# A decoder layer's feed-forward: the down projection of three chunks by seven half-size products, its sums accumulated in DRAM by transfers

## The chip, the cores and the metric

One NeuronCore of a Trainium2 chip runs the whole program. The metric is the device time of one execution in microseconds (us), the median of the runs. Engines are named as the profile names them: PE is TensorE, DVE is VectorE, ACT is ScalarE, POOL is GpSimd, SP is SyncE, which here only issues transfers.

## The reference

A decoder layer over x of 8 x 100 tokens by 1024, all in float32: a retention block, a cross attention with 722 context positions, and a gated feed-forward of hidden width 4096, each followed by an addition of the residual and a layer normalisation. The change touches the feed-forward, whose input x is the normalised output of the attention block:

```
h   = silu(x @ w_gate.T) * (x @ w_up.T)        # 800 x 4096
y   = x + h @ w_down.T                         # 800 x 1024
out = layernorm(y)
```

## The kernel before, in words

Everything is kept transposed: a tensor of 800 tokens by 1024 features stands as 128 partitions x 8 tiles (k) x 800 columns. A float32 product is made of three matmuls in fp32r: weights and operand are split into a high part (ACT copies, rounding) and a low part (DVE subtracts the high part from the original), and PE multiplies high x high, high x low and low x high.

The feed-forward (`phase_tail`, from line 3368) goes over 4 chunks of 1024 hidden features (`CHUNKS`). A chunk has two stages.

*Gate and up* (56 products, lines 3641 to 3684). The chunk's 8 tiles of hidden features are made in four couples of two; a couple takes a gate block (even block b) and an up block (odd b). Each block is a 2 x 2 block product by the seven-product scheme of Strassen and Winograd: 7 products, each of 4 k-tiles x 3 passes = 12 matmuls of 400 columns (`QUAD = 4`, `HALF = 400`), in place of 8. The moving operands (`MOVING`) are quarters of x and four sums of quarters ("sides"), made once. The stationary ones are quarters of a pair of weight units in `RAW`, and sums of them, made by DVE ("mixes", line 3958, four a block). What PE is given as weights are "entries": 512 columns of high part made by ACT (line 3821) and of low part by DVE (line 4062), in a ring of four slots. So the entry of product n may be begun when product n - 4 is done. The results stand in three PSUM banks a block, and are put together by DVE with five additions ("combines": u2, u3, c22, c21, c12, line 4105) and one ACT copy (`keep`, line 3873). Products 4, 6 and 7 open or add to a bank that an earlier combine or keep must have read. ACT applies silu (line 3867), DVE multiplies gate by up (m11, m22, m21, m12, line 4119). The result G (two tiles x 800) is split into `HH` (ACT, line 3852) and `HL` (DVE, line 4073), the hidden operand.

*Down* (lines 3700 to 3717). Eight output units, each of 8 k-tiles x 2 column parts (512 and 288 columns) x 3 passes = 48 matmuls, plain. DVE adds each unit's two banks to the residual `c.R` in SBUF (line 4134). Weight units are split whole, 1024 columns at a time (lines 3838, 4068). The last chunk's down stage goes by halves of the columns, interleaved with the closing normalisation (`down_by_halves`); it is another function.

Nothing is planned by a scheduler: each engine has its list of instructions written out by hand in `chunk` (PE line 3742, ACT line 3875, DVE line 4158), executed strictly in that order, with waits on counting semaphores (`f_hi`, `f_lo` for entries, `f_done` for products, `outs` for combines and multiplications, `kept`, `h_hi`, `h_lo`, `t_sum`, `t_hi`, `t_lo`). SP issues the load of each pair of weight units (1 MB, line 3516) when the low part of an entry two pairs back is made. POOL does nothing in the feed-forward but one memset (line 3505). In the retention phase POOL issues transfers that add in place (line 1716), as it does for the value weights (`add_raw`, line 112).

Of the kernel before, what the change touches and what calls it, by code (L numbers as in the profile page):

```python
# [65 lines left out]
ENTRIES = 8 * PRODUCTS + 2 * KT  # L66
# [103 lines left out]
def phase_context(c, nc, sem):  # L170

    with ExitStack() as ctx:
# [1123 lines left out]
        done.wv_mix = wv_mix  # L1296
        c.minus, c.MINUS = wv_hi, 8
# [232 lines left out]
def phase_retention(c, nc, sem, before, norm):  # L1530


    with ExitStack() as ctx:
# [135 lines left out]
        def sync(sp):  # L1669
# [1698 lines left out]
def phase_tail(c, nc, sem_of, attention):  # L3368
# [4 lines left out]
    with ExitStack() as ctx:  # L3373
# [5 lines left out]
        def below(words, *tiles, dtype=F32):  # L3379

            with ExitStack() as room:
# [17 lines left out]
        kept_parts.append(below("t_wo6_", (FLAT, UNIT), (0, UNIT), dtype=F32R))  # L3399
        ROOM = sb("ROOM", [P, AFTER], F32R)  # L3400
        G = sb("G", [P, 2, NT])
        U2, U3, CT = (sb(n, [P, HALF]) for n in ("U2", "U3", "CT"))
        S3 = sb("S3", [P, QUAD * P])
        (x_hi, x_lo, added, gated, freed, h_hi, h_lo, stored, f_hi, f_lo, f_done, s_op, outs, silu,
         t_sum, t_hi, t_lo, r_add, ones_made, kept) = (sem(n) for n in (
             "x_hi", "x_lo", "added", "gated", "freed", "h_hi", "h_lo", "stored", "f_hi", "f_lo",
             "f_done", "s_op", "outs", "silu", "t_sum", "t_hi", "t_lo", "r_add", "ones_made", "kept"))
# [26 lines left out]

        MOVING = (operand(0, 0), side(2), side(1), side(3), operand(1, 0), side(4), operand(1, 1))
        BANK = (0, 1, 2, 1, 0, 1, 2)
        OPENS = (True, True, True, True, False, True, False)

# [5 lines left out]
        def block_source(b, p):  # L3444

            if p == 3:
                return S3[:]
            return raw_pair(b)[:, (0, 0, 2, None, 1, 3, 1)[p], :]
# [7 lines left out]

        def down_unit(t, n):
            if t == LAST:
                return last_down(n)
            return c.WH[:, n % 2, :], c.WL[:, n % 2, :]  # L3460
# [42 lines left out]
        def gpsimd(pool):  # L3503
            pool.wait_ge(f_done, PER * LAST + 56)
            pool.memset(ones[:], 1.0 / D).then_inc(ones_made, 1)

        def sync(sp):
            weight_stream(c, sp, U_WO // 2 + 2, (U_FFN - U_WO) // 4 + 1)

            def load(t, i):  # L3510

                before = (PER * t + 7 * (i - 1) if 2 <= i < 10 else
                          PER * t + 56 + 4 * (i - 9) if i >= 10 else
                          PER * t - 4 * (2 - i) + 4)
# [3 lines left out]

            def chunk(t, first, last):
# [10 lines left out]
            sp.wait_ge(stored, 16 * KT)  # L3530
# [59 lines left out]
        def tensor(pe):  # L3590
# [50 lines left out]
            def product(t, b, p, first):  # L3641
                couple, up = b // 2, b % 2
                base = 14 * couple + 5 * up
                if p == 0:
# [10 lines left out]
                    if first and b == 2:  # L3655
                        pe.wait_ge(gated, 2)
# [804 lines left out]
```

## Time and profile before

| | us |
|---|---|
| median of 3 runs (lowest, highest) | 2628.17 (2628.12, 2628.95) |
| the profiled execution, its own time | 2627.58 |
| its span in the profile | 2625.8 |
| PE busy | 2593.7 (99%) |
| DVE busy | 1811.0 (69%) |
| ACT busy | 1200.9 (46%) |
| POOL busy | 24.2 (1%) |

The span is the stretch from the first to the last instruction of the profiled execution; its own time is 1.8 us more. Matmul records are pipelined and overlap, so the pace of PE is the distance between starts, not the mean duration of a record. The feed-forward's chunks begin at about 1867, 2030.7, 2223.0 and 2415.4 us; the first has only six blocks, since its first couple is made before it.

### The profile page before, as it was taken

The numbers are of one execution on the slowest core, as the hardware profiler recorded it, in microseconds if no ns is written. First come the engines' busy times: TensorE is split into PE (matmuls) and PEld (weight loads), VectorE is DVE, ScalarE is ACT, GpSimd is POOL, SyncE is SP. The second block draws the span as 40 slices with busy tenths as digits, with TensorE's granted clock in tenths as the row PEclk, the third lists the DMA queues.
The fourth block names the chain that finished last, engine by engine and source line by source line (L and its number), as shares of the span: only waits on it lengthen the run. The fifth ranks groups of instructions, "written<-read, shape, count | busy, mean of one in ns | idle before, by whom it ended". The sixth has DMA issues, their size and how long they took to land.

```text
span 2625.8 us, 41672 instructions
## 1 busy us (share of the span) xinstructions
PE 2593.7 (99%) x16328; PEld 2458.0 (94%) x16328; DVE 1811.0 (69%) x2502; ACT 1200.9 (46%) x2047; POOL 24.2 (1%) x37
## 2 busy tenths in 40 slices
PE   9999999999999999999999999999999999999998
PEld 9999999999999988998889999899998999999997
DVE  7777776687777764867788888736973763763766
ACT  6555555555444433444466666522531431431441
POOL 0000000000000000000000000000000000000000
PEclk9999999999999999999999999999999999999999
DMA  5444445422212231344256666421121121211121
GB/s 198 159 145 161 149 135 179 148 78 60 73 57 77 62 90 52 94 106 93 75 143 174 174 170 166 106 76 55 47 81 48 65 81 49 81 65 65 65 80 51
DMA packets 138765, 264.79 MB, mean 101 GB/s; under 512 B 25076, under 2 KB 98284, under 8 KB 125676
## 3 DMA queue, kind: packets, MB, share of 16 engines
q1 hardware_dynamic: 136108, 255.53, 31.5%
q0 software_dynamic: 2496, 7.01, 1.5%
q8 instruction: 113, 1.85, 0.3%
q14 instruction: 48, 0.39, 0.0%
HBM read 198.24 MB, written 57.26 MB: 97 GB/s over the span
## 4 chain that ended last, share of the span: by engine, by line
PE 94%; DVE 3%; ACT 1%; issue 1%; DMA 0%; DVEq 0%; POOL 0%; SPq 0%; ACTq 0%; POOLq 0%
PE PS L3680 6%; PE PS L3678 6%; PE PS L3682 6%; PE PS L3151 5%; PE PS L149 4%; PE PS L147 4%; PE PS L148 4%; PE PS L2526 3%; PE PS L2528 3%; PE PS L2524 3%; PE PS L3164 3%; PE PS L1181 3%; PE PS L1183 3%; PE PS L1185 3%; PE PS L1144 3%; PE PS L1146 3%
## 5 line engine op out<-in xcount | busy, mean ns | idle before, releaser
L3821 ACT ACTIVATE WH<-RAW 128x512 fp32r<-128x512 f32 x180 | 113.5, 632 | 222.1 <-PE PS L3682 119.4
L149 PE MATMUL PS<-XH,WL 128*128 128x512 f32 (+1 forms) x592 | 204.4, 345 | 0.0
L147 PE MATMUL PS<-XH,WH 128*128 128x512 f32 (+1 forms) x592 | 204.1, 345 | 0.0
L4062 DVE TENSOR_TENSOR WL<-RAW,WH 128x512 fp32r<-128x512 f32 x196 | 134.7, 688 | 58.8 <-ACT WH L3821 55.5
L148 PE MATMUL PS<-XL,WH 128*128 128x512 f32 (+1 forms) x496 | 170.1, 343 | 0.0
L3680 PE MATMUL PS<-XL,WH 128*128 128x400 f32 x480 | 166.0, 346 | 0.0
L3678 PE MATMUL PS<-XH,WH 128*128 128x400 f32 x480 | 164.8, 343 | 0.8 <-issue 0.6
L3682 PE MATMUL PS<-XH,WL 128*128 128x400 f32 x480 | 165.0, 344 | 0.0
L3323 DVE TENSOR_TENSOR XL<-PS,XH 128x400 fp32r<-128x400 f32 (+2 forms) x224 | 122.6, 571 | 56.3 <-ACT XH L3256 51.7
L3256 ACT ACTIVATE XH<-PS 128x400 fp32r<-128x400 f32 (+2 forms) x224 | 106.4, 507 | 95.9 <-PE PS L3164 95.9
L1745 ACT ACTIVATE WH<-RAW 128x512 fp32r<-128x512 f32 x132 | 81.8, 632 | 132.3 <-DVE RAW L2046 79.5
L3716 PE MATMUL PS<-t_ROOM,WL 128*128 128x512 f32 (+1 forms) x384 | 132.5, 345 | 0.0
L3715 PE MATMUL PS<-t_ROOM,WH 128*128 128x512 f32 (+1 forms) x384 | 131.7, 343 | 0.0
L3714 PE MATMUL PS<-t_ROOM,WH 128*128 128x512 f32 (+1 forms) x384 | 131.6, 343 | 0.0
L3304 DVE TENSOR_REDUCE a_LOW<-PS 100x1 f32<-100x824 f32 x128 | 129.7, 1014 | 2.5
L3678 PE MATMUL PS<-t_ROOM,WH 128*128 128x400 f32 x360 | 124.4, 345 | 0.3 <-issue 0.3
L1181 PE MATMUL PS<-WALL,WH 128*128 128x256 f32 x448 | 124.5, 278 | 0.0
L1183 PE MATMUL PS<-WALL,WL 128*128 128x256 f32 x448 | 124.3, 277 | 0.0
L1185 PE MATMUL PS<-WALL,WH 128*128 128x256 f32 x448 | 124.2, 277 | 0.0
L3680 PE MATMUL PS<-t_ROOM,WH 128*128 128x400 f32 x360 | 124.1, 345 | 0.0
L3682 PE MATMUL PS<-t_ROOM,WL 128*128 128x400 f32 x360 | 123.9, 344 | 0.0
L149 PEld LDWEIGHTS PS<-XH,WL 128*128 128x128 f32 x592 | 111.3, 188 | 12.3
(536 smaller groups left out, 8168.7 us busy)
## 6 DMA issues: line engine op xcount, KB each, us to landing
RAW<-weights_dram SPq DMA_DIRECT2D x100, 1024.0 KB, 4.9
values_scratch<-VS SPq DMA_DIRECT2D x44, 512.0 KB
a_KHL<-keys_scratch SPq DMA_DIRECT2D x32, 411.0 KB, 5.1
RAW<-context_dram SPq DMA_DIRECT2D x6, 2048.0 KB, 8.9
XH<-values_scratch SPq DMA_DIRECT2D x16, 640.0 KB
XL<-values_scratch SPq DMA_DIRECT2D x16, 640.0 KB
R<-context_dram SPq DMA_DIRECT2D x4, 2048.0 KB, 9.3
keys_scratch<-KS SPq DMA_DIRECT2D x16, 512.0 KB, 3.9
```

Source lines behind the costliest of these rows:

```text
L147: pe.matmul(out, wh, xh[:, k, cols], start=(k == 0), stop=False)
L148: pe.matmul(out, wh, xl[:, k, cols], start=False, stop=False)
L149: mm = pe.matmul(out, wl, xh[:, k, cols], start=False, stop=(k == KT - 1))
L1181: pe.matmul(out, hi[:, k, cols], wh, start=(opens and t + k == 0), stop=False, skip_group_check=True)
L1183: pe.matmul(out, lo[:, k, cols], wh, start=False, stop=False, skip_group_check=True)
L1185: mm = pe.matmul(out, hi[:, k, cols], wl, start=False, stop=(k == QUAD - 1), skip_group_check=True)
L3678: pe.matmul(out, wh, high[:, k, :], start=(OPENS[p] and k == 0), stop=False, skip_group_check=True)
L3680: pe.matmul(out, wh, low[:, k, :], start=False, stop=False, skip_group_check=True)
L3682: mm = pe.matmul(out, wl, high[:, k, :], start=False, stop=(k == QUAD - 1), skip_group_check=True)
L3715: pe.matmul(out, wh, HL[:, k, cols], start=False, stop=False)
L3716: mm = pe.matmul(out, wl, HH[:, k, cols], start=False, stop=(i == KT - 1))
L4062: dve.tensor_tensor(ring[1][:, e % RING, :], src, ring[0][:, e % RING, :].bitcast(F32), ALU.subtract).then_inc(f_lo, 1)
```

## The change

In chunks 0, 1 and 2 the down projection becomes four blocks (`DOWN_BLOCKS`) of seven products each, through the same function as the gate and up blocks (`strassen`), with the same ring of entries and the same mixes of weights. Its moving operands (`HIDDEN`) are quarters of the hidden operand and four sums of them, made per couple by DVE (`hidden_sum`), then split by ACT (`hidden_side_hi`) and DVE (`hidden_side_lo`). Sums 1 need the first two couples, sums 2, 3 and 4 the last two. A down block's results are put together by three ACT copies (`keep_down`) and five DVE additions (`combine_down`) in G, two tiles x 800.

The place of the residual in SBUF is needed for the sums: `c.HSIDE` has the addresses of `c.R`. So the normalised x is stored to DRAM (`rscr`) by SP (`keep_residual`), each down block's two tiles are added to it there by accumulating transfers that POOL issues (`send`), and before the last down stage it is fetched back (`fetch_residual`). G is free for the next block when the transfer has landed (`SENT`). u2 and u3 of the gate blocks now stand in U2 and U3 instead of G.

In the retention phase a load of SP gets one wait more. The last chunk's gate, up and down stages do the work of before.

```
+DOWN_BLOCKS = KT // 2
+BLOCKS = 8 + DOWN_BLOCKS
-ENTRIES = 8 * PRODUCTS + 2 * KT
+ENTRIES = BLOCKS * PRODUCTS
...
                 sp.wait_ge(f_lo, F_LO + PER * (i - 1) + 14)
+                sp.wait_ge(roped, 2 * i + 1)
                 load_pair(pair_of(i, 3))
...
+        HIDDEN = (hidden(0, 0), hidden_side(2), hidden_side(1), hidden_side(3), hidden(1, 0),
+                  hidden_side(4), hidden(1, 1))
+        DOWN_ORDER = (0, 2, 1, 4, 3, 6, 5)
...
+            def send(t, d, tile):
+                if t == 0 and d == 0:
+                    pool.wait_ge(stored, STORED)
+                if t > 0 or d > 0:
+                    pool.wait_ge(SENT[tile], sent(t, d - 1, tile))
+                pool.dma_start(c.rscr[:, 2 * d + tile, :], G[:, tile, :],
+                               accum_op=ALU.add).then_inc(SENT[tile], 16)
+            for t in range(LAST):
+                for d in range(DOWN_BLOCKS):
+                    pool.wait_ge(kept, down_kept(t, d, 3))
+                    pool.wait_ge(outs, down_outs(t, d, 4))
+                    send(t, d, 0)
+                    pool.wait_ge(outs, down_outs(t, d, 5))
+                    send(t, d, 1)
...
+            def fetch_residual():
+                sp.wait_ge(f_done, PER * LAST)
+                for tile in range(2):
+                    sp.wait_ge(SENT[tile], sent(LAST - 1, DOWN_BLOCKS - 1, tile))
+                for k in range(0, KT, 2):
+                    sp.dma_start(c.R[:, k:k + 2, :], c.rscr[:, k:k + 2, :]).then_inc(stored, 16)
             def chunk(t, first, last):
                 for i in range(4 if first else 0, 12):
+                    if last and i == 4:
+                        fetch_residual()
                     load(t, i)
+            keep_residual()
...
+            def down_product(t, d, q):
+                if q == 0:
+                    if d == 0:
+                        pe.wait_ge(h_lo, KT * t + 4)
+                        pe.wait_ge(outs, OUTS * t + (14 * 3 + 5))
+                        pe.wait_ge(silu, 16 * t + 14)
+                    elif d == 1:
+                        pe.wait_ge(outs, OUTS * t + GATES)
+                    else:
+                        pe.wait_ge(outs, down_outs(t, d - 2, 5))
+                        pe.wait_ge(kept, down_kept(t, d - 2, 3))
+                if q == 3:
+                    pe.wait_ge(kept, down_kept(t, d, 1))
+                if q == 4:
+                    pe.wait_ge(outs, down_outs(t, d, 1))
+                if q == 5:
+                    pe.wait_ge(kept, down_kept(t, d, 2))
+                if q == 6:
+                    pe.wait_ge(outs, down_outs(t, d, 2))
+                if d == 0 and q == 3:
+                    pe.wait_ge(h_lo, KT * t + KT)
+                if d == 0 and q in (1, 2, 4, 6):
+                    pe.wait_ge(t_lo, side_parts(t, {1: 2, 2: 6, 4: 7, 6: 8}[q]))
+                strassen(t, 8 + d, q, HIDDEN)
...
+            def keep_down(t, d, which):
...
+                    act.wait_ge(f_done, PER * t + (56 + PRODUCTS * d + 4))
+                    if d == 0:
+                        act.wait_ge(t_sum, side_sums(t, SUMS))
+                        act.wait_ge(h_lo, KT * t + KT)
+                    else:
+                        act.wait_ge(SENT[0], sent(t, d - 1, 0))
+                    out, x = G[:, 0, 0:HALF], bank(0)
...
+            def combine_down(t, d, which):
...
+                elif which == "u3":
+                    dve.wait_ge(f_done, PER * t + at + 5)
+                    dve.wait_ge(outs, down_outs(t, d, 1))
+                    out, x, y = U3[:], U2[:], bank(1)
...
```

DVE's list in a gate block that follows a finished couple (`ended`), and in the down stage:

```
                     entry_lo(t, e)
-                    if inner and not up:
-                        hidden_lo(t, couple - 1, 1)
+                    if not last and ended in (0, 1):
+                        hidden_sum(t, 1, ended)
+                    if not last and ended == 2:
+                        hidden_sum(t, 2, 2)
+                    if ended is not None:
+                        hidden_lo(t, ended, 1)
                     entry_lo(t, e + 1)
                     if not (first and b == 2):
                         mix(t, b, 3)
-                    if inner and not up:
-                        hidden_lo(t, couple - 1, 0)
+                    if not last and ended == 2:
+                        hidden_sum(t, 3, 2)
                     combine(t, b, "u2")
...
                         entry_lo(t, e + 2)
+                        if not last and ended == 2:
+                            hidden_sum(t, 4, 2)
+                        if ended is not None:
+                            hidden_lo(t, ended, 0)
...
+                    for d in range(DOWN_BLOCKS):
...
+                        if d == 0:
+                            last_part(t, 7)
+                            hidden_sum(t, 2, 3, 0)
+                            hidden_sum(t, 3, 3, 0)
+                            hidden_sum(t, 4, 3)
+                            hidden_side_lo(t, 2, 3)
+                            entry_lo(t, e)
+                            hidden_lo(t, 3, 1)
+                            hidden_lo(t, 3, 0)
+                            entry_lo(t, e + 1)
+                            combine_down(t, d, "u2")
+                            hidden_side_lo(t, 3, 3)
+                            mix(t, b, 3)
+                            entry_lo(t, e + 2)
+                            hidden_side_lo(t, 4, 3)
+                            entry_lo(t, e + 3)
+                            mix(*following, 0)
+                            mix(*following, 1)
+                        else:
+                            combine_down(t, d - 1, "c21")
+                            entry_lo(t, e)
+                            entry_lo(t, e + 1)
+                            mix(t, b, 3)
+                            mix(*following, 0)
+                            mix(*following, 1)
+                            entry_lo(t, e + 2)
+                            combine_down(t, d, "u2")
+                            entry_lo(t, e + 3)
+                        entry_lo(t, e + 4)
+                        mix(*following, 2)
+                        combine_down(t, d, "u3")
+                        combine_down(t, d, "c22")
+                        entry_lo(t, e + 5)
+                        combine_down(t, d, "c12")
+                        entry_lo(t, e + 6)
```

Later in a gate block come the lows of the sides: `hidden_side_lo(t, 1, ended)` after couples 0 and 1, `hidden_side_lo(t, 2, 2)`, `(t, 3, 2)` and `(t, 4, 2)` in block 6; in block 7 the sums 2 and 3 of the last couple's second tile. ACT's list has the matching high parts, `keep_down` "u", "ct" and "c11" ahead of a down block's entries 1, 2 and 4, and in block 0 of the down stage `hidden_hi(t, 3, 1)`, the entry, `hidden_side_hi(t, 2, 3)`, `hidden_hi(t, 3, 0)`, then one side high after each of the next two entries.

## Rows read from the trace of the kernel before

**Rows 1.** The page, part 1: engines, busy us, share of the span, instructions.

```profile
PE 2593.7 (99%) x16328; PEld 2458.0 (94%) x16328; DVE 1811.0 (69%) x2502; ACT 1200.9 (46%) x2047; POOL 24.2 (1%) x37
```

**Rows 2.** Table by stage: chunk 1's products, then its down projection.

```profile
core 0: us, PE busy (x) PEld busy (x) DVE busy (x) ACT busy (x) POOL busy (x), PEclk, DMA share, GB/s
2030.68:2153.40 122.72, 122.72 (x674) 122.28 (x673) 92.61 (x147) 50.40 (x87) 0.00 (x0) 1.00 0.20 69
2153.40:2223.03 69.63, 69.63 (x386) 61.45 (x385) 21.11 (x23) 9.80 (x11) 0.00 (x0) 1.00 0.18 61
```

**Rows 3.** Waits of PE, 1867 to 2538: who waited for whom, us, times, longest.

```profile
PE PS L3678 <- issue: 0.8, 2, 0.6
PE PS L3678 <- DVE WL L4062: 0.2, 1, 0.2
```

**Rows 4.** Groups by line and form, chunk 1: busy, mean ns | idle before.

```profile
L4062 DVE TENSOR_TENSOR WL<-RAW,WH 128x512 fp32r<-128x512 f32 x52 | 35.8, 688 | 16.4 <-ACT WH L3821 15.5
L3958 DVE TENSOR_TENSOR RAW<-RAW 128x512 f32<-128x512 f32 x24 | 16.6, 692 | 0.8
L4105 DVE TENSOR_TENSOR t_G<-t_G,PS 128x400 f32<-128x400 f32 x16 | 9.1, 571 | 6.1 <-PE PS L3682 5.9
L4073 DVE TENSOR_TENSOR t_ROOM<-t_G,t_ROOM 128x800 fp32r<-128x800 f32 x8 | 7.8, 985 | 0.0
...
L3852 ACT ACTIVATE t_ROOM<-t_G 128x800 fp32r<-128x800 f32 x8 | 6.8, 860 | 0.0
```

**Rows 5.** Timeline of DVE from the end of block 5: start, us, what.

```profile
2122.90 0.57 DVE L4105 TENSOR_TENSOR t_CT<-t_U,PS 128x400 f32<-128x400 f32 x1 [0.42 <-PE PS L3682]
2123.51 0.57 DVE L4119 TENSOR_TENSOR t_G<-t_CT,t_G 128x400 f32<-128x400 f32 x1
...
2127.48 0.98 DVE L4073 TENSOR_TENSOR t_ROOM<-t_G,t_ROOM 128x800 fp32r<-128x800 f32 x1
2128.59 0.57 DVE L4105 TENSOR_TENSOR t_G<-t_U,PS 128x400 f32<-128x400 f32 x1
2129.08 0.69 DVE L4062 TENSOR_TENSOR WL<-RAW,WH 128x512 fp32r<-128x512 f32 x1
2129.68 0.68 DVE L3958 TENSOR_TENSOR t_S<-RAW 128x512 f32<-128x512 f32 x1
2130.40 0.69 DVE L3958 TENSOR_TENSOR RAW<-RAW 128x512 f32<-128x512 f32 x1
...
2131.71 1.18 DVE L4105 TENSOR_TENSOR t_G<-t_G,PS 128x400 f32<-128x400 f32 x2
...
2155.30 1.89 DVE L4073 TENSOR_TENSOR t_ROOM<-t_G,t_ROOM 128x800 fp32r<-128x800 f32 x2
```

**Rows 6.** Timeline of PE, block 6: first two matmuls of product 4.

```profile
2129.25 0.42 PE L3678 MATMUL PS<-t_ROOM,WH 128*128 128x400 f32 x1
2129.51 0.34 PE L3680 MATMUL PS<-t_ROOM,WH 128*128 128x400 f32 x1
```

**Rows 7.** DMA issues: KB each, median us to landing; last, line 1716's own.

```profile
RAW<-weights_dram SPq DMA_DIRECT2D x100, 1024.0 KB, 4.9
a_KHL<-keys_scratch SPq DMA_DIRECT2D x32, 411.0 KB, 5.1
...
VW<-RAW POOLq DMA_DIRECT2D x4, 512.0 KB, 4.6
...
keys_scratch<-KS SPq DMA_DIRECT2D x4, 420.0 KB, 3.3
...
DMA to landing us min/median/max: 3.1/3.6/7.2
```

**Rows 8.** Timelines of SP, POOL and DVE, retention, first head loop.

```profile
574.51 0.33 SPq L1677 DMA_DIRECT2D RAW<-weights_dram  x1
...
570.91 1.80 POOL L1716 DMA_DIRECT2D T<-T  x2 [569.75 <-DVE T L2118]
...
584.47 0.68 DVE L2046 TENSOR_TENSOR S<-RAW 128x512 f32<-128x512 f32 x1
```

More of the change, by code:

```diff
@@ L3913, in chunk @@
                                 gate(t, couple, "s11")
-                if last:
-                    act.preload_act_table_set("natural_log_exp_and_others")
-                for n in range(2 * KT if last else KT):
+                if not last:
+                    for d in range(DOWN_BLOCKS):
+                        for q in range(PRODUCTS):
+                            if q == 0 and d == 0:
+                                hidden_hi(t, 3, 1)
+                            if q == 1:
+                                keep_down(t, d, "u")
+                            if q == 2:
+                                keep_down(t, d, "ct")
+                            if q == 4:
+                                keep_down(t, d, "c11")
+                            entry_hi(t, 56 + PRODUCTS * d + q + 3)
+                            if q == 0 and d == 0:
+                                hidden_side_hi(t, 2, 3)
+                                hidden_hi(t, 3, 0)
+                            if d == 0 and q in (1, 2):
+                                hidden_side_hi(t, q + 2, 3)
+                    return
+                act.preload_act_table_set("natural_log_exp_and_others")
+                for n in range(2 * KT):
                     if n == 0:
@@ L4173, in chunk @@
                     inner = b > (2 if first else 0)
-                    ahead = b < 7
+                    ahead = b < 7 or not last
+                    ended = couple - 1 if inner and not up else None
                     e = PRODUCTS * b + 3
                     if b == 0:
-                        add_rows(t - 1, KT - 1)
-                        entry_lo(t, 2)
+                        combine_down(t - 1, DOWN_BLOCKS - 1, "c21")
                     if inner:
@@ L4216, in chunk @@
                         times(t, couple, "m22")
+                        if not last and couple == 3:
+                            hidden_sum(t, 2, 3, 1)
+                            hidden_sum(t, 3, 3, 1)
+                        if first and b == 3:
+                            for each in range(2):
+                                first_hidden_sum(each)
+                    elif not last and ended in (0, 1):
+                        hidden_side_lo(t, 1, ended)
+                    elif not last and ended == 2:
+                        hidden_side_lo(t, 2, 2)
                     entry_lo(t, e + 5)
@@ L4220, in chunk @@
                         times(t, couple, "m21")
-                    entry_lo(t, e + 6)
+                        if first and b == 3:
+                            hidden_side_lo(t, 1, 0)
+                    elif not last and ended == 2:
+                        hidden_side_lo(t, 3, 2)
+                        hidden_side_lo(t, 4, 2)
+                    entry_lo(t, e + 6)
+                if not last:
+                    for d in range(DOWN_BLOCKS):
+                        b, e = 8 + d, 56 + PRODUCTS * d + 3
+                        following = (t, b + 1) if d < DOWN_BLOCKS - 1 else (t + 1, 0)
+                        if d == 0:
[16 more added lines that the diff above has]
+                            mix(*following, 1)
+                        else:
+                            combine_down(t, d - 1, "c21")
[14 more added lines that the diff above has]
+                        entry_lo(t, e + 6)
+                    return
                 last_part(t, 7)
```

459 lines of the change are left out of this document (282 added, 177 removed).

## The prediction

> **What bounds the kernel now.** The page's engine line [rows 1] has TensorE busy 99% of the span and VectorE 69%. A busy PE is not a PE at its peak, so the table by stage is read next. It is cut at the starts of chunk 1's first gate product, its first down matmul and the next chunk's first product: the gate and up products take 122.72 us, the down projection 69.63 us [rows 2]. In both PE is busy throughout at a granted clock of 1.00, the higher of its two levels; the other engines differ: VectorE is busy 75% of the first stretch and 30% of the second. The waits of PE over all four chunks' products hold 1 us [rows 3]. So TensorE's own pace is the bound, and VectorE is the engine with the least room.
>
> The pace comes from the length of these stretches, not from mean durations, since pipelined records overlap. 122.72 us for 56 products of 12 matmuls is 0.1826 us per 128x400 matmul and 2.19 us per product; 69.63 us for 384 matmuls averaging 400 columns is 0.1813 us each.
>
> **TensorE's part.** Per chunk 0 to 2 the 384 down matmuls (8 units x 8 k x 2 column parts x 3 passes) become 4 blocks x 7 products x 4 k x 3 passes = 336 matmuls of 400 columns. They issue from the statement that the gate products issue from, so they cost 336 x 0.1826 = 61.4 us against 69.6: 8.3 us less a chunk, 24.8 us in three, if nobody is late. Weight loads fall 384 to 336 with the columns, 400 to a load before and after. Chunk 3 keeps its down projection.
>
> **What VectorE and ScalarE get in exchange.** Added per chunk on VectorE: 28 low entries and 16 mixes of 512 columns, 20 combines of 400, 10 operand sums and 8 operand lows of up to 800; gone are 4 + 6x2 half-unit lows and 8 row adds of 800. By durations [rows 4] the new chunk holds about 157 us of VectorE work (84 entries 58, 48 mixes 33, 76 ops of 400 43, 4 hidden lows of 400 and 4 of 800 6, ten sums 8, eight side lows 8), where now it is busy 93 + 21 = 114 us, in 184 us of PE time. On average it fits. What decides is where it stands, because a chunk's sums can only be made when its last couples are done.
>
> I step through the queues by the distance of neighbouring starts, not by durations, since the records overlap by about 0.08 us: 0.49 us for a 400 op and 0.61 when the next one needs its result; 0.60 and 0.72 for a 512 op; 0.90 and 1.11 for an 800 op [rows 5]. A product may start without a gap if what it waits for ended 0.39 us before the signal of the product ahead. That comes from one row pair: the combine ("u2") at 2128.59 ended at 2129.15; the product that waits for its bank has its first two matmuls 0.26 us apart instead of 0.18, so it is 0.08 late, while the product ahead signals at 2122.90 + 3 x 2.19 = 2129.46 [rows 5, 6]; 2129.15 + 0.39 - 2129.46 = 0.08.
>
> Block 6 (clock 0 = end of block 5, products end every 2.19). Before its second combine ("u3") VectorE now has: c12 and m12 1.1, entry 0.6, a sum 0.9, hidden low 0.9, entry 0.7, mix 0.6, second sum 0.9, u2 0.5, entry 0.6, third sum 0.9, hidden low 0.9, two mixes 1.3, entry 0.6. u3 starts at 10.6 and ends at 11.1; before it started at 8.8 [rows 5]. The sixth product wants its bank at 10.95 - 0.39: about 0.5 us lost. Block 7, with two 400 sums, gains it back in its own waits, and VectorE enters the down stage 0.4 us late.
>
> Down block 0 (clock 0 = end of block 7). VectorE: c12, m12, two single-tile sums, one 800 sum; the low of side 2 starts at 3.7 and ends at 4.7. ScalarE has its high part by 3.1, so it is not late. The third product wants it at 4.38 - 0.39: 0.7 us lost. Two hidden lows follow, ended at 7.1 where the fourth product wants them at 6.9: 0.2 us. Then entry, u2, side 3's low, mix, an entry that waits 0.7 us for ScalarE's high part, side 4's low, entry, two mixes, entry, mix: u3 starts near 15.3 and ends at 15.9, while the seventh product wants its bank at 13.6 (six products, the 0.9 us lost so far, less 0.39): 2.3 us. Together 3.2 us. Blocks 1 to 3 carry 7 entries, 4 mixes, 5 combines, 10.4 us in 15.3, and lose nothing; block 0 of the next chunk likewise. Blocks 2 and 4 trade an 800 low before u2 for a sum and a 400 low and lose nothing. Against the 0.1 us a block like 6 loses already, a chunk loses 3.6 us, three lose 10.8. ScalarE itself is busy 50 of 123 us [rows 2]; its additions (12 keeps, 8 side highs of up to 0.86 [rows 4], 12 more half-entries net) fit, but its queue is in order, which matters below.
>
> **The accumulating transfers.** No row shows one that ends in DRAM. Nearest are 512 KB sums in SBUF, 4.6 us to landing, and 200 KB ones, 3.1 to 7.2 us; a plain 420 KB store took 3.3 us, a plain 411 KB load 5.1 us [rows 7]. The new ones carry 400 KB. Lower bound 3.3 us, upper 7.2 us, or the load and the store one after the other, 8.4 us; I take 5 us, nearest the 512 KB rows. They have cover: tile 0 is complete 0.6 us after the sixth product and is wanted by ScalarE (c11) after the next block's fourth, 10.9 - 0.6 = 10.3 us; tile 1 has about 11 us, and 8.2 us at the end of a chunk, where the gate block's combines come earlier. Behind a late c11 stands that block's next high entry, with 1 us to spare. So up to 8.2 us the price is nothing, and at 8.4 us still nothing that is seen.
>
> The Trainium skill, "Collectives: The Full Stack", section on why ReduceScatter is half of AllGather, says an adding transfer reads two sources and so moves its bytes at half the rate. The 512 KB sum above took 4.6 us where a plain load of 1024 KB took 4.9 [rows 7], so this case's trace agrees about the rate; and if the rule is laid on the 411 KB load it gives an estimate of 10.2 us, with which the sum would still be what it is, the cover nearly used up.
>
> **The rest.** The 8 residual stores leave SP's queue after the normalised tiles and ahead of the load of pair 4, which anyhow waits for the seventh entry of block 2; weights arrive in 4.9 us against a 15 us block [rows 7]. The fetch of 3.2 MB stands ahead of pair 4 in chunk 3, with two blocks of slack, and is used 120 us later. Price nothing; if the cover were gone, 17 us once (four loads like the 4.9 us one, one by one, less overlap). The new wait on the first head loop's fourth load: the load went out at 574.51, the sum behind its wait was issued at 570.91 and lands about 3.6 later, so the load goes 1 us late, is 5 us long and is first read at 584.47 [rows 7, 8]. Nothing.
>
> **Sum.** 2627.58 us of the profiled execution (span 2625.8 and 1.8 around it) - 24.8 + 10.8 = 2613.6. The profiled execution is 0.6 us under the median of the runs, so 2614.2 as a median.
>
> **Rivals.**
> (1) All of it is hidden, the gain is 24.8 us: 2603.4. For it: the ring of four entries lets VectorE be up to 4.9 us late with an entry (three products, less 1.3 us to make it and the 0.39). Against: u3 and side 2's low are not entries, they have one product of slack. Chance 0.12.
> (2) VectorE's queue costs twice what I step through (a stall in block 6 carried into block 7 and the down stage): 3 x 7.2 = 21.6 us back, 2625.0, within what can be told apart from no change. Chance 0.08.
> (3) Slower: the accumulating transfer is the new bound. Place: ScalarE's c11 in down blocks 1 to 3, and VectorE's c22 in the next chunk's block 0; both stand at the head of in-order queues with the entries behind them. With landing time L it costs 9 x (L - 11.3) + 3 x (L - 11.0); it cancels my gain of 14.0 us at L = 12.3. At three times the 512 KB row, 13.8 us, it costs 31 us: 2645. Against it: every transfer row is under 8. Chance 0.06.
> The forecast holds 0.74, from 2608 (stalls of 1.5 us a chunk) to 2621 (6 us).
>
> **Numbers.** 0.2% is 5.3 us, about what a measurement of this kernel can tell from no change. Faster 0.88 (forecast, rival 1 and the good edge of rival 2), same 0.06, slower 0.06. The range 2603 to 2622 takes in rival 1 and leaves out (2)'s centre and (3).
>
> **What would show it.** Gate stretches as now near 122.7 us plus 0.5; down stretches of chunks 0 to 2 near 64.6 us, of which 61.4 PE; PE waits of some 0.7 and 2.3 us in the third and seventh product of down block 0, released by VectorE (the low of side 2, then u3); no wait of ScalarE on the transfers. Landing times over 11 us, or down stretches over 69 us, make it wrong; stretches of 61.5 us make rival 1 right.

## The result, and the profile after

The changed kernel takes 2611.06 us (median of 4 runs, 2610.54 to 2611.18); the kernel before took 2628.14 us on the same chip (4 runs, 2627.91 to 2628.95). The ratio is 0.9935, 95% interval 0.9922 to 0.9947: 17.1 us less. The forecast was 2614.2 us, 3.1 us above it. As the following shows, several things that the forecast did not have lie behind that small difference, and the two largest, both of them effects outside the products themselves, point in opposite directions.

First the page of the kernel after, its engine line and the transfers of the residual. They answer to [rows 1] and [rows 7].

```profile
PE 2573.4 (99%) x16184; PEld 2459.5 (94%) x16184; DVE 1912.8 (73%) x2695; ACT 1258.6 (48%) x2168; POOL 45.0 (2%) x61
...
residual_scratch<-t_G POOLq DMA_DIRECT2D x24, 400.0 KB, 5.1
```

TensorE has 144 matmuls fewer (3 x 48) and is still busy 99%; VectorE has 193 instructions and 102 us more. The time lies where it lay before, in TensorE's pace, so the next view is the table by stage: chunk 1's products and its down projection, answering to [rows 2], and four short stretches that the text comes to.

```profile
core 0: us, PE busy (x) PEld busy (x) DVE busy (x) ACT busy (x) POOL busy (x), PEclk, DMA share, GB/s
2022.56:2145.62 123.06, 122.87 (x673) 122.35 (x673) 100.22 (x161) 53.62 (x93) 0.96 (x2) 1.00 0.23 76
2145.62:2211.40 65.78, 63.45 (x338) 62.42 (x338) 47.31 (x75) 26.00 (x45) 6.01 (x7) 0.97 0.44 102
...
1974.00:1977.60 3.60, 3.60 (x13) 3.60 (x12) 2.44 (x5) 0.63 (x1) 0.86 (x1) 0.53 0.36 28
...
2159.30:2161.80 2.50, 0.49 (x4) 0.16 (x2) 2.33 (x4) 1.15 (x2) 0.00 (x0) 1.00 0.90 259
2161.80:2165.30 3.50, 3.50 (x11) 3.46 (x12) 2.26 (x4) 0.11 (x1) 0.86 (x1) 0.51 0.27 115
...
2350.60:2354.00 3.40, 3.40 (x19) 3.40 (x20) 3.12 (x6) 0.76 (x2) 0.94 (x2) 1.00 0.27 113
```

The gate and up stretch grew by 0.34 us (forecast 0.5). The down stretch fell from 69.63 to 65.78 us (forecast near 64.6), and its mean granted clock is 0.97 instead of 1.00. That third number had no place in the forecast.

Who is late for whom is in the waits of PE from 1860 to 2540 us, which answer to [rows 3] (waiting engine, released by; us in total, times, longest):

```profile
PE PS L3740 <- DVE t_U L4348: 6.0, 3, 2.0
PE PS L3740 <- DVE HSIDE L4272: 1.0, 3, 0.3
...
PE PS L3740 <- DVE t_U L4311: 0.7, 4, 0.2
```

The stalls have the names and the places that were forecast: u3 (line 4348) 2.0 us once in each of three chunks, the low of side 2 (line 4272) 0.3, and block 6's second combine (line 4311, three times). The fourth wait on line 4311 has no place in the forecast: in chunk 0, block 3, the fourth product waits for the first combine (u2), and its start at 1886.10 us comes 0.51 us behind the one before. The recorded wait is shorter than the loss, because the record before it still runs. The loss is read from starts: in the timeline of PE the third and the seventh product of chunk 1's down block 0.

```profile
2149.80 0.34 PE L3744 MATMUL PS<-HSIDE,WL 128*128 128x400 f32 x1
2150.47 0.45 PE L3740 MATMUL PS<-HSIDE,WH 128*128 128x400 f32 x1 [0.32 <-DVE HSIDE L4272]
2150.76 0.34 PE L3742 MATMUL PS<-HSIDE,WH 128*128 128x400 f32 x1
...
2159.36 0.34 PE L3744 MATMUL PS<-t_ROOM,WL 128*128 128x400 f32 x1
2161.72 0.60 PE L3740 MATMUL PS<-t_ROOM,WH 128*128 128x400 f32 x1 [2.01 <-DVE t_U L4348]
2162.12 0.54 PE L3742 MATMUL PS<-t_ROOM,WH 128*128 128x400 f32 x1
2162.45 0.54 PE L3744 MATMUL PS<-t_ROOM,WL 128*128 128x400 f32 x1
```

Starts are 0.67 us and 2.36 us apart where 0.18 to 0.19 is the pace: 0.48 and 2.17 us lost. The start after such a one is late too, here by another 0.11 us (0.29 apart). Behind the long gap the next starts are 0.40 and then 0.33 us apart instead of 0.18. This is the lower level of the clock: the stretch from 2161.80 has a granted clock of 0.51 with TensorE busy throughout, the 2.50 us ahead of it 1.00 with TensorE nearly idle. Chunk 0 shows the same (1974.00, clock 0.53), there from about 1.2 us after TensorE went on at 1972.88; chunk 2 has a gap of the same size, and none of it (2350.60, clock 1.00).

The timeline of DVE in the same block tests the step through its queue (clock 0 of the forecast is 2146.0):

```profile
2156.17 0.69 DVE L4218 TENSOR_TENSOR WL<-RAW,WH 128x512 fp32r<-128x512 f32 x1 [0.76 <-ACT WH L3925]
...
2158.45 0.69 DVE L4117 TENSOR_TENSOR t_S<-RAW 128x512 f32<-128x512 f32 x1
2159.16 0.69 DVE L4117 TENSOR_TENSOR RAW<-RAW 128x512 f32<-128x512 f32 x1
2159.78 0.68 DVE L4218 TENSOR_TENSOR WL<-RAW,WH 128x512 fp32r<-128x512 f32 x1
2160.49 0.69 DVE L4117 TENSOR_TENSOR RAW<-RAW 128x512 f32<-128x512 f32 x1
2161.10 0.56 DVE L4348 TENSOR_TENSOR t_U<-t_U,PS 128x400 f32<-128x400 f32 x1
```

u3 starts 15.1 us after the clock 0, where 15.3 was forecast; the entry's wait for ScalarE is 0.76 us (0.7 forecast). Right ahead of u3 stand three mixes for the next block, which nobody wants yet.

**The part outside the feed-forward.** Its first product starts at 1862.14 us, before at 1867.27: 5.1 us of the gain are there before any changed product has run. They come in the main from one place near 940 us, the last head loop of the retention phase. Waits of all engines from 900 to 970 us, before:

```profile
ACT QK L1804 <- POOLq L1719: 8.2, 1, 8.2
...
PE PS L2385 <- DVE R L2135: 4.5, 1, 4.5
```

The same view after:

```profile
ACT QK L1808 <- POOLq L1723: 4.1, 1, 4.1
...
PE PS L2389 <- DVE R L2139: 0.3, 1, 0.3
```

And the issues there, from the timelines of SP and POOL, before:

```profile
933.18 0.33 SPq L1677 DMA_DIRECT2D RAW<-weights_dram  x1
...
932.81 0.83 POOL L1716 DMA_DIRECT2D T<-T  x1 [2.53 <-issue]
```

and after:

```profile
937.01 7.81 SPq L1680 DMA_DIRECT2D RAW<-weights_dram  x2
...
933.81 0.83 POOL L1720 DMA_DIRECT2D T<-T  x1 [2.54 <-issue]
```

Before, SP sent a 1 MB weight load 0.4 us behind POOL's 200 KB sum, and the sum landed after 7.2 us, the maximum of line 1716 in [rows 7]. After, the added wait holds the load back until the sum has landed, which takes 3.1 us, and ScalarE, VectorE and TensorE behind it go on 4 us earlier.

The wait is not the whole price. Behind the 4.5 us gap of the kernel before stands the lower clock, in a view of PE alone:

```profile
core 0: us, PE busy (x), PEclk, DMA share, GB/s
946.70:951.20 4.50, 4.50 (x14) 0.51 0.87 230
```

The 13 starts from 946.68 to 951.18 us take 4.50 us, where the same shapes (six of 512 columns, six of 288, one of 512) take 2.41 at the pace of the rows around them: 2.1 us more. The kernel after has clock 1.00 there. So the place is worth 4.1 us of gap and 2.1 us of clock, 6.2 us. Of these 5.1 are left at the first product because the profiled execution of the kernel after came to this place 1.0 us later than that of the kernel before (938.67 against 937.68 us, the first matmul on PE's line 2389, before 2385); it is there at the first accumulating sum already (571.91 against 570.91 us), ahead of the added wait's first use, and it differs between executions: run 3, whose program is the same up to there, reaches the later place at 937.96 us.

### The profile page after: what moved, and what is told of

Read it like the earlier page. It is cut to its first block, busy times and chain, and to the rows that moved or that the text cites. A ratio compares the mean times of both kernels' runs of the same rounds, so it can differ in the third digit from the quotient of the medians.

```text
span 2608.9 us, 42024 instructions
## 1 busy us (share of the span) xinstructions
PE 2573.4 (99%) x16184; PEld 2459.5 (94%) x16184; DVE 1912.8 (73%) x2695; ACT 1258.6 (48%) x2168; POOL 45.0 (2%) x61
## 4 chain that ended last, share of the span: by engine, by line
PE 90%; DVE 6%; issue 2%; ACT 1%; DMA 0%; DVEq 0%; POOL 0%; SPq 0%; ACTq 0%; POOLq 0%
PE PS L3740 7%; PE PS L3742 7%; PE PS L3744 7%; PE PS L3155 5%; PE PS L151 4%; PE PS L149 4%; PE PS L150 4%; PE PS L2530 3%; PE PS L2532 3%; PE PS L2528 3%; PE PS L3168 3%; PE PS L1183 3%; PE PS L1185 3%; PE PS L1187 3%; PE PS L1146 3%; PE PS L1148 3%
## 5 line engine op out<-in xcount | busy, mean ns | idle before, releaser
L3925 ACT ACTIVATE WH<-RAW 128x512 fp32r<-128x512 f32 x252 | 158.5, 630 | 253.2 <-PE PS L3744 168.3
L4218 DVE TENSOR_TENSOR WL<-RAW,WH 128x512 fp32r<-128x512 f32 x256 | 176.0, 688 | 61.8 <-ACT WH L3925 56.3
L3740 PE MATMUL PS<-t_ROOM,WH 128*128 128x400 f32 x552 | 191.9, 348 | 6.5 <-DVE t_U L4348 6.0
L3742 PE MATMUL PS<-t_ROOM,WH 128*128 128x400 f32 x552 | 191.5, 347 | 0.0
L3744 PE MATMUL PS<-t_ROOM,WL 128*128 128x400 f32 x552 | 191.0, 346 | 0.0
L1749 ACT ACTIVATE WH<-RAW 128x512 fp32r<-128x512 f32 x132 | 81.8, 631 | 130.4 <-DVE RAW L2050 74.0
L102 DVE TENSOR_TENSOR WL<-RAW,WH 128x1024 fp32r<-128x1024 f32 x40 | 49.0, 1225 | 104.5 <-ACT WH L96 100.1
L151 PEld LDWEIGHTS PS<-XH,WL 128*128 128x128 f32 x592 | 111.3, 188 | 12.3
L1146 PE MATMUL PS<-WH,WALL 128*128 128x256 f32 x440 | 122.7, 279 | 0.0
L1148 PE MATMUL PS<-WL,WALL 128*128 128x256 f32 x440 | 122.5, 279 | 0.0
```

Source lines behind the costliest of these rows:

```text
L151: mm = pe.matmul(out, wl, xh[:, k, cols], start=False, stop=(k == KT - 1))
L1146: pe.matmul(out, wh, hi[:, k, :], start=(opens and j + k == 0), stop=False, skip_group_check=True)
L1148: pe.matmul(out, wh, lo[:, k, :], start=False, stop=False, skip_group_check=True)
L3740: pe.matmul(out, wh, high[:, k, :], start=(OPENS[p] and k == 0), stop=False, skip_group_check=True)
L3742: pe.matmul(out, wh, low[:, k, :], start=False, stop=False, skip_group_check=True)
L3744: mm = pe.matmul(out, wl, high[:, k, :], start=False, stop=(k == QUAD - 1), skip_group_check=True)
```

## The experiments

**1 and 2. The retention wait alone, both ways.** Theory: the added wait in the retention phase is worth 5 us by itself. Rival: the 5 us belong to something else of the change. First the kernel before with the wait added:

```diff
                 sp.wait_ge(f_lo, F_LO + PER * (i - 1) + 14)
+                sp.wait_ge(roped, 2 * i + 1)
                 load_pair(pair_of(i, 3))
```

> The kernel before with one line more: the load of the fourth weight pair of each head loop in the retention phase waits for the rotation of that loop's first tile. Theory A (the wait keeps a 1 MB weight load from getting in front of an accumulating transfer in the last head loop, where the trace of before shows 7.2 us to landing and a 4.5 us stall of TensorE, and the trace of after neither): 2628.1 - 5.1 = 2623.0 us, and the 4.5 us stall gone. Rival B (the 5.1 us by which the changed kernel reaches its feed-forward earlier come from the moved memory or semaphores, not from the wait): 2628 us, stall unchanged. Rival C (what I had forecast, the wait costs and gains nothing): 2628 us as well.

Measured: 2622.15 us (10 runs) against 2628.23 (14 runs), ratio 0.9976 (0.9967 to 0.9986), 6.1 us less. TensorE's wait from 900 to 970 us:

```profile
PE PS L2386 <- DVE R L2136: 0.3, 1, 0.3
```

The converse, the kernel after without that line:

> The changed kernel without that one wait. Theory A: the 4.5 us stall of TensorE at the last head loop comes back, 2611.1 + 5.1 = 2616.2 us, and the feed-forward itself is as in the changed kernel, 11.8 us shorter than before. Rivals B and C: 2611 us. If both e1 and e2 move by 5 us, the parts add up and the down projection's own gain is 12 us, not 17.

Measured: 2616.77 us (5 runs), ratio 0.9957 (0.9943 to 0.997), 5.7 us more than the kernel after. TensorE's wait from 900 to 970 us, and below it the table by stretches, behind the long gap of chunk 0, then behind that of chunk 2:

```profile
PE PS L2388 <- DVE R L2138: 4.5, 1, 4.5
```

```profile
1979.50:1982.50 3.00, 3.00 (x11) 2.96 (x10) 1.60 (x4) 0.15 (x1) 0.86 (x1) 0.50 0.26 31
...
2354.70:2357.70 3.00, 2.98 (x9) 2.95 (x10) 2.26 (x4) 0.21 (x1) 0.65 (x1) 0.54 0.33 139
```

Added to one kernel or taken from the other, the wait moves the same 4 us of waits and 5.7 to 6.1 us of time; the rest is the clock behind the gap, which has 0.50 at 946 to 950 us in run 2 and 1.00 in run 1. That is shown. The second table adds that here the lower clock stands behind the gaps of chunks 0 and 2; in the kernel after it was chunks 0 and 1. The gaps are the same 2 us, so length alone does not decide it.

**3. The long gap closed.** In down block 0, u3, an entry and c22 go ahead of the three mixes.

```diff
                             entry_lo(t, e + 3)
-                            mix(*following, 0)
-                            mix(*following, 1)
+                            combine_down(t, d, "u3")
+                            entry_lo(t, e + 4)
+                            combine_down(t, d, "c22")
+                            for n in range(3):
+                                mix(*following, n)
```

> The changed kernel with VectorE's list in down block 0 reordered: u3, the next entry and c22 stand ahead of the three mixes. Theory D (the seventh product waits 2.2 us for u3, behind work that is not urgent, and the gap also lowers the granted clock to 0.5 for 3.4 us in two of three chunks, 1.6 us each): 3 x 2.2 + 2 x 1.6 = 9.8 us less, 2601.3 us, and no stretch under clock 1.00 in the down stages. Rival E (the clock falls there whatever the gap): 3 x 2.2 = 6.6 us less, 2604.5, the half-clock stretches remain. Rival F (VectorE is overloaded in that block, so the time comes back at the next wait): 2608 or more.

Measured: 2600.41 us (2600.22 to 2600.6, 4 runs), ratio 0.9894 (0.9879 to 0.9909). In the waits of PE the line of u3 is gone, what is left is as before:

```profile
PE PS L3740 <- DVE HSIDE L4272: 1.0, 3, 0.3
```

10.7 us less than the kernel after, for 6.0 us of recorded waits (6.5 by starts, 6.8 with the late start behind each). 3.3 us of the rest is the clock, whose lower stretches are gone: its mean over the core goes from 0.997 to 0.999. Another 0.8 us has nothing to do with the edit: the same product of chunk 0 starts at 1868.31 us here and at 1869.11 in the kernel after, before either has done anything different.

**4. The other stalls too.** Run 3, and in block 6 the third sum behind an entry and the fourth behind c22, in down block 0 the third sum behind the hidden lows (the counts of the waits follow):

```diff
-                    if not last and ended == 2:
-                        hidden_sum(t, 3, 2)
                     combine(t, b, "u2")
...
                         if not last and ended == 2:
-                            hidden_sum(t, 4, 2)
+                            hidden_sum(t, 3, 2)
...
                         combine(t, b, "c22")
+                        if not last and ended == 2:
+                            hidden_sum(t, 4, 2)
...
                             hidden_sum(t, 2, 3, 0)
-                            hidden_sum(t, 3, 3, 0)
...
                             hidden_lo(t, 3, 0)
+                            hidden_sum(t, 3, 3, 0)
```

> As e3, and the operand sums 3 and 4 of block 6 stand behind u2 and u3, and sum 3 of down block 0 behind side 2's low and the hidden lows. Theory D: besides e3's gain the 0.35 us stall of the sixth product of block 6 and the 0.5 us stall of the third product of down block 0 go, the fourth's grows from 0.2 to about 0.4 us: 3 x 0.7 = 2 us less than e3, 2599.3 us. Rival F: same as e3 or slower, as the moved sums are late for their own products.

Measured: 2598.92 us (2598.59 to 2599.76, 4 runs), ratio 0.9889 (0.9873 to 0.9904). This is the fastest version here, 29 us under the kernel before and 12 under the kernel after. What PE still waits for of the combines:

```profile
PE PS L3740 <- DVE t_U L4311: 0.2, 1, 0.2
```

In chunk 1's down block 0 the first starts of the third, fourth and fifth product are still 0.36, 0.33 and 0.40 us behind the ones before them, so 0.18, 0.15 and 0.22 us lost; one sum moved from ahead of side 2's low to behind it makes the fifth late, which was not.

**5. The long gap shortened only.** Here u3, the entry and c22 go ahead of the third mix alone, so that a gap of about 0.7 us should stay. Theory: the lower clock follows only the long gap. Rival: it follows any gap there.

```diff
                             mix(*following, 1)
+                            combine_down(t, d, "u3")
+                            entry_lo(t, e + 4)
+                            combine_down(t, d, "c22")
+                            mix(*following, 2)
```

> The changed kernel with u3 and c22 of down block 0 moved ahead of the third mix only, behind the first two: VectorE reaches u3 1.3 us earlier, so the gap of TensorE ahead of the seventh product shrinks from 2.0 us to 0.7. Theory D (a gap of 2 us lowers the granted clock, a shorter one does not): 3 x 1.3 + 2 x 1.6 = 7.1 us less than the changed kernel, 2604.0 us, clock 1.00 all through the down stages. Rival (any gap in this place lowers it): 3.9 us less, 2607.2 us, matmuls 0.33 us apart behind the gap in some chunk.

Measured: 2603.37 us (2602.98 to 2603.79, 4 runs) against 2628.54, ratio 0.9905 (0.9889 to 0.9922). The waits of PE and the mean granted clock of the core:

```profile
PE PS L3740 <- DVE t_U L4348: 2.0, 3, 0.7
```

```profile
core 0: 2600.8 us, clock 0.999
```

The waits fell by 4.0 us, the time by 7.7. Three gaps of 0.7 us cost 3.0 us against run 3 (2.7 if each run is taken against its own runs of before) and left the clock alone, at 0.999 in all four executions and 1.00 behind each gap of the profiled one; three of 2.0 us cost 10.7, or 9.9 without the 0.8 us above. The gaps alone would be 2.8 and 6.8 us by starts; what makes the long ones dearer is the clock. The rival's 2607.2 is out.

**6, 7 and 8. Is the accumulating transfer covered, and what if not?** Theory: the cover of 8 to 11 us holds, the residual's way through DRAM costs nothing. Rival: the transfer is near the bound. Run 6 gives each send one more plain transfer of 400 KB, from the same tile to a tensor that is not read, ahead of the adding one and counted in the same semaphore.

```diff
                     pool.wait_ge(SENT[tile], sent(t, d - 1, tile))
+                for n in range(1):
+                    pool.dma_start(c.more[:, 2 * n + tile, :], G[:, tile, :]).then_inc(SENT[tile], 16)
                 pool.dma_start(c.rscr[:, 2 * d + tile, :], G[:, tile, :],
```

> The changed kernel, and ahead of each accumulating transfer a plain one of the same 400 KB from the same tile into a DRAM tensor that nobody reads, counted in the same semaphore. POOL issues 0.87 us later and a transfer lands when both have: 5.1 us become about 8. Theory G (the transfers have 8.2 us of cover at a chunk's end, 10.3 in a down block, and 1 to 2.8 us of slack behind it): no change, 2611 us. Rival H (the transfers are already the last to arrive): 2611 + 12 x 3 = 2647 us.

Measured: 2609.39 us (2608.14 to 2610.43, 4 runs), ratio 0.9929 (0.9912 to 0.9946): no loss. From the page, the two transfers, then POOL's timeline in the last down block of chunk 0, and the table of PE alone (columns as at 946.70) behind the 2.0 us gaps of chunks 0 and 1:

```profile
more_scratch<-t_G POOLq DMA_DIRECT2D x24, 400.0 KB, 2.8
residual_scratch<-t_G POOLq DMA_DIRECT2D x24, 400.0 KB, 5.2
```

```profile
2022.28 0.57 POOL L3567 DMA_DIRECT2D more_scratch<-t_G  x1 [0.44 <-DVE t_G L4350]
2026.61 0.85 POOL L3568 DMA_DIRECT2D residual_scratch<-t_G  x1 [3.76 <-DVE t_U L4313]
```

```profile
1971.90:1975.00 3.10, 3.10 (x10) 0.51 0.19 79
2160.40:2163.80 3.40, 3.40 (x19) 1.00 0.26 109
```

The landing times are hardly longer, yet the cover was used: POOL, with no wait of the program between the two lines, issues the adding transfer of tile 1 4.3 us after the plain one, where the two of tile 0 go out 0.6 us apart, so it lands later by the difference, and VectorE's c22 in the next chunk's block 0 waits for it (line 4313, 3 times, at most 1.0 us), with TensorE not behind it. Run 6 came out 1.7 us under the kernel after. This need not be a gain by its edit: of its three gaps of 2.0 us only chunk 0's was followed by the lower clock, and its feed-forward was reached 1.3 us earlier. Its four executions lie at 2608.1 and 2608.4 us (mean clock 0.998) and twice at 2610.4 (0.997), 2 us apart for one kernel.

Run 7 makes them two (`range(2)`):

> As e6 with two plain transfers ahead of each. The two tiles of a block follow each other by 2.2 us in one queue, so the second lands some 13 us after its data are complete, and the 16 engines are busy nearly the whole block. Theory G: its cover of 11 + 1 us in a down block holds or is missed by 1 us, that of 8.2 + 2.8 us at the end of a chunk is missed by 2 us: 2611 + 6 to 2611 + 18, so 2617 to 2629 us, the first waits of ScalarE or VectorE on the transfers, at the first block of the next chunk. Rival H: 2680 us.

Measured: 2654.52 us (2653.9 to 2655.37, 4 runs), ratio 1.0099 (1.0082 to 1.0115). The waits from 1860 to 2540 us, then POOL's timeline in the last down blocks of chunk 0:

```profile
DVE t_G L4350 <- DMA residual_scratch<-t_G: 43.2, 8, 7.0
DVE t_G L4313 <- DMA residual_scratch<-t_G: 29.1, 3, 10.0
...
PE PS L3742 <- DVE t_G L4313: 19.7, 3, 6.8
...
PE PS L3742 <- DVE WL L4220: 12.5, 7, 3.2
```

```profile
2016.21 0.95 POOL L3568 DMA_DIRECT2D residual_scratch<-t_G  x1
2016.77 0.95 POOL L3567 DMA_DIRECT2D more_scratch<-t_G  x1
2022.48 0.54 POOL L3567 DMA_DIRECT2D more_scratch<-t_G  x1 [4.76 <-issue]
```

Run 8 makes each adding transfer twice, the second after the first has landed, so that the output holds the down products of chunks 0 to 2 twice.

```diff
-                pool.dma_start(c.rscr[:, 2 * d + tile, :], G[:, tile, :],
-                               accum_op=ALU.add).then_inc(SENT[tile], 16)
+                for n in range(2):
+                    if n:
+                        pool.wait_ge(SENT[tile], sent(t, d, tile) - 32 + 16 * n)
+                    pool.dma_start(c.rscr[:, 2 * d + tile, :], G[:, tile, :],
+                                   accum_op=ALU.add).then_inc(SENT[tile], 16)
```

> The changed kernel with each accumulating transfer made twice, one after the other, each waited for by POOL: the output then holds each down product of chunks 0 to 2 twice. POOL's chain is 4 transfers of 5.2 us, 20.8 us, to a block of 15.3 us, so the transfers set the pace. Theory G: the first block hides it, the second is late by 4 us, every further one and the first of the next chunk by about 5.5: some 18 us a chunk, 2611 + 54 = 2665 us. If it comes out under 2630 the queue has more room than I count; a clock that falls in the gaps would put it over 2670.

Measured: 2707.98 us (2706.03 to 2709.76, 4 runs), ratio 1.0304 (1.0287 to 1.0321). From the same view of the waits:

```profile
DVE t_G L4351 <- DMA residual_scratch<-t_G: 62.8, 9, 8.2
...
ACT t_G L4014 <- DMA residual_scratch<-t_G: 35.7, 8, 9.0
...
PE PS L3743 <- DVE t_G L4314: 28.0, 3, 10.0
```

Run 6 shows that the cover holds one plain transfer more. Runs 7 and 8 show the stall when it is gone, in part where rival 3 had it: the next chunk's block 0 (line 4313 in run 7, 4314 in run 8), and ScalarE's c11 (line 4014 in run 8). The largest wait, though, is VectorE's in the down blocks themselves (line 4350 in run 7, 4351 in run 8), where c22 and c12 write G, and behind it its low entries, for which TensorE waits in run 7 another 12.5 us (line 4220).

Both lost much more than was expected of them: 43 us over the kernel after against 6 to 18 for run 7, and 97 against 54 for run 8. Of the 43 us of run 7, TensorE's own recorded waits have 32.2 (19.7 and 12.5), and the lower clock about 8: in the feed-forward 75 matmuls of 400 columns run at the lower level, where the kernel after has 18, at some 0.15 us each. In run 8 the added waits come to 70.6 us, and 126 matmuls run at the lower level, some 16 us more than in the kernel after. Why the transfers were so late is less clear. Part of it shows in POOL's rows, where the second plain transfer of tile 1, behind four transfers just issued, goes out 5.7 us after the one ahead of it, as run 6 showed with 4.3 us. How much is this hold at the issue, and how much the two tiles' transfers lengthening each other, was not taken apart.

## Why the prediction was right, and where it was not

**What bounds it.** Right. TensorE's pace sets the end before and after, and of the engines only VectorE made it wait in the changed stages.

**TensorE's part.** Right. In the other down blocks of chunk 1 a block of 84 matmuls takes 15.27 us, 0.1818 us each against 0.1826 forecast. That is 3 x (69.63 - 336 x 0.1818) = 25.6 us less, where the sum had 24.8.

**VectorE's order.** Right in place and nearly in size in the blocks that were named; one stall more stands in chunk 0's block 3, which the forecast did not step through (0.33 us at 1886.10, and 0.11 behind it). Per chunk, measured against forecast: block 6, 0.35 against 0.5 us; third product of down block 0, 0.48 against 0.7; fourth, 0.16 against 0.2; seventh, 2.17 against 2.3. Together 3.2 against 3.7 us, 9.5 us in three chunks. Run 3 shows cause and remedy, since the order of the same instructions alone brought 9.9 of the 10.7 us. What the forecast was off in is VectorE's load: its 157 us a chunk is a sum of durations, and it was set beside 93 + 21 = 114 us of busy time, in which overlapping records count once. Measured in the same way the chunk went from 113.7 to 147.5 us, 34 us more and not 43. The steps by starts were free of this, and carried the forecast.

**A missing term: the clock behind a gap.** The step that failed is "2.3 us" as the whole price of the seventh product's stall. The forecast took a stalled TensorE to resume at the pace it had. In two of three chunks it ran at the lower level for about 3.4 us; some eleven matmuls at 0.33 instead of 0.18 us make 1.6 us each time, 3.3 us in all. The feed-forward of the kernel before has no gap of that length [rows 3], but its retention phase has one: 4.5 us near 944 us, and behind it the clock at 0.51 (the row of 946.70 above), for 2.1 us. So the trace at hand had a row for the price of a long gap, and could not say that a gap of 2.0 us is enough.

**The account of the feed-forward.** Measured: the last down projection starts at 2521.18 us, before at 2538.10. Of these 16.9 us, 5.1 were there at the start, so the feed-forward gained 11.8 us where the forecast had 14.0. From the parts: 25.6 - 9.5 - 3.3 = 12.8. The late start behind each stall (0.07 to 0.12 us, twelve times) takes 1.1 us more, the stall in chunk 0's block 3 another 0.4, which gives 11.3: the parts agree to half a microsecond.

**The retention wait.** The step that failed is "Nothing". The forecast read the first head loop alone, where the load goes 1 us late at no cost [rows 8], and took it for all. The row that spoke against it was among those shown: line 1716's landing has a minimum of 3.1 and a maximum of 7.2 us [rows 7], and the maximum belongs to the sum that TensorE's 4.5 us wait hangs on. Runs 1 and 2 show 5.7 to 6.1 us for it. About 4.1 us of it is the gap and 2.1 the clock behind it. The change brought these, but not by its products; the kernel before could have had them alone. The landing time was the sign and not the cost: a sum issued at 654.78 us landed after 7.1 us as well, still took 7.0 in the kernel after, and TensorE has no wait from 650 to 680 us in the kernel before.

**The transfers.** Right. Landing was taken at 5 us; the row of line 3566 (minimum, median, maximum):

```profile
DMA to landing us min/median/max: 4.7/5.1/6.9
```

It is below the 8.2 us of the shortest cover, no engine but POOL waits for it (once, 4.5 us), and run 6, whose adding transfer goes out some 4 us later at a chunk's end, shows room for that. The forecast had weighed the Trainium skill, "Collectives: The Full Stack", section on why ReduceScatter is half of AllGather: an adding transfer reads two sources and moves its bytes at half the rate. It was laid on the 411 KB load there, giving an estimate of 10.2 us, which the 5.1 us disprove. Run 6 has a better row for it, a plain transfer of the same tile from the same queue, 2.8 us against 5.2: against its own kind the adding one does take nearly twice as long, as the page would have it. That is a ratio of times from issue to landing, and not of rates, which no run here separates; with three transfers for each tile (run 7) it is 6.1 to 4.0. So the landing times of run 6 agree with the rule, and the row it was laid on was of another kind. The forecast's agreement, 512 KB added at 4.6 us and 1024 KB plain at 4.9, hung on the choice of the row too: against the 411 KB load of 5.1 us, in the same rows, the sum would not be slower at all.

**The rivals.** Rival 1 (2603.4, all hidden) did not come, yet 2598.92 in run 4 is below it, with the retention's gain and nearly all stalls gone. Rival 2 (twice the stalls) was wrong about VectorE's queue. Its idea, that a stall costs more than its own length, was right of the clock. Rival 3 (slower) did not come. By its formula its gain of 14.0 us is gone at L = 12.4, not 12.3. The formula, one landing time against one cover, treats a tile by itself; with both tiles' transfers in one POOL queue it falls short by a wide margin, as runs 7 and 8 show.

**The number.** 2611.06 lies in the range of 2603 to 2622. Against the forecast's 14.0 us it has 5.1 us that came from ahead of the feed-forward, a gain not forecast, and 2.2 us less from the feed-forward itself, mostly the 3.3 us that the clock took back. That both were left out and are of opposite sign is why the total came out better than it would have with the retention gain alone; this closeness is luck.

## What to carry to other kernels

Where the bound engine is 99% busy and another is asked to do more beside it, walk through that engine's queue once with the due time of each item: here an operation wanted at once stood behind three wanted by the next block, and the exchange of their places was worth about 10 us, nearly as much as the changed products had brought in the end (11.8). When a wait is added in a loop, look at its worst instance and not at its first; a landing time whose maximum is twice its minimum is a reason to look, and what decides is whether the bound engine's own wait hangs on it. And price a long gap of TensorE with the clock behind it, which a trace of before may already show in another phase: here a gap of 2.0 us cost 2.3 us by itself and 1.6 more in five places of nine.

## What the runs showed of the hardware that was not expected

- A gap of 2.0 us in a TensorE busy 99% was followed by 3.1 to 3.5 us at a granted clock of 0.5 (the 1.2 GHz level) in two places of three in the kernel after and in run 2, and in one of three in run 6; which chunk is spared differs. The fall came at once behind the gap (chunk 1 of the kernel after) or 1.2 us later (chunk 0). Gaps of 0.7 us (run 5, three) never were followed by it. A gap of 4.5 us was in the kernel before and in run 2. What decides it between equal gaps is open.
- A 200 KB accumulating transfer in SBUF landed in 7.2 to 7.3 us where a 1 MB weight load from another queue was issued 0.4 us after it (the kernel before, run 2), and in 3.1 us where the load came 3 us later (the kernel after, run 1).
- A 400 KB transfer from SBUF to DRAM landed in 2.8 us plain (run 6) and in 5.1 us adding. With three behind each other for each tile the medians were 4.0 plain and 6.1 adding (run 7).
- POOL stood idle at an issue with no wait of the program before it: 4.5 to 4.8 us behind four such transfers (run 7), and 3.8 us behind three (run 6).
